# Scores of the first self attention on row halves of the array, weighted sums in pairs, projections from split rows

## What is computed

```python
h = _layernorm(x, ln1_g, ln1_b)
q = (h @ wq).reshape(B, S, 16, 64)      # wk, wv alike
attn = jnp.einsum('bihd,bjhd->bhij', q, k) * 64 ** -0.5
attn = jax.nn.softmax(attn, axis=-1)
out = jnp.einsum('bhij,bjhd->bihd', attn, v).reshape(B, S, 1024)
x = out @ wo + bo + x
```

## Time and profile before

| | us |
|---|---|
| median of 3 runs | 2029.41 (2028.31 to 2030.17) |
| profiled execution, its own time | 2027.02 |
| its span | 2025.3 |
| granted TensorE clock, mean | 0.964 |
| PE busy | 1851.6 (91%) |
| DVE busy | 1157.2 (57%) |
| POOL busy | 879.0 (43%) |
| ACT busy | 781.4 (39%) |

### The profile page before, as it was taken

The page is one execution under the profiler, slowest core; times in us unless marked ns, Lnnn a source line. Parts: engine busy times, 40 slices in busy tenths (PEclk is TensorE's granted clock), DMA queues, the critical chain, the costliest instruction groups (busy, mean ns, idle before and its releaser), DMA issues. The chain is left out here.

```text
span 2025.3 us, 27798 instructions
## 1 busy us (share of the span) xinstructions
PE 1851.6 (91%) x8972; PEld 1078.1 (53%) x8972; DVE 1157.2 (57%) x2195; ACT 781.4 (39%) x1300; POOL 879.0 (43%) x767
## 2 busy tenths in 40 slices
PE   4999999999999999979899999996798976898799
PEld 1444444444444444438555577885444434665678
DVE  4666666666666666633566433244688853687601
ACT  2344444444444443441344313221266663344340
POOL 2366666666666666661122300111146655366110
PEclk9999999999999999989999899997699998999899
DMA  1422222232323232203000001103244421000001
GB/s 52 107 62 53 61 54 67 62 70 62 70 62 70 62 70 62 63 24 94 24 1 1 1 3 48 28 10 53 51 70 77 87 48 28 9 1 1 29 16 42
DMA packets 64798, 93.99 MB, mean 46 GB/s; under 512 B 20992, under 2 KB 47132, under 8 KB 64703
## 3 DMA queue, kind: packets, MB, share of 16 engines
q1 hardware_dynamic: 60351, 86.20, 18.9%
q0 software_dynamic: 4352, 6.56, 1.5%
HBM read 22.84 MB, written 2.24 MB: 12 GB/s over the span
## 5 line engine op out<-in xcount | busy, mean ns | idle before, releaser
L1181 POOL TENSOR_TENSOR x<-x,sa_p_buf 128x1024 f32<-128x1024 f32 x192 | 455.2, 2371 | 165.7 <-ACT sa_p_buf L1029 157.7
L1029 ACT ACTIVATE sa_p_buf<-sa_score 128x512 f32<-128x512 f32 x512 | 277.7, 595 | 304.7 <-PE sa_score L956 304.5
L1092 DVE TENSOR_REDUCE sa_mx<-sa_front 128x1 f32<-128x512 f32 x512 | 319.4, 680 | 98.9 <-PE sa_front L930 98.9
L956 PE MATMUL sa_score<-sa_q_stage,sa_k_stage 128*128 128x512 f32 x1024 | 323.9, 438 | 0.0
L970 PE MATMUL sa_out<-sa_p_buf,sa_v_buf 128*64 128x512 f32 x1024 | 275.7, 617 | 0.0
L956 PEld LDWEIGHTS sa_score<-sa_q_stage,sa_k_stage 128*128 128x128 f32 x1024 | 177.8, 189 | 102.9 <-issue 71.3
L528 ACT ACTIVATE sa_p_buf<-sa_score 128x1024 f32<-128x1024 f32 (+1 forms) x160 | 141.1, 938 | 89.9 <-PE sa_score L476 89.8
L1668 POOL TENSOR_TENSOR x<-x,bias_out 128x1024 f32<-128x1024 f32 x24 | 55.7, 2348 | 275.5 <-POOLq L1853 239.3
L342 DVE TENSOR_REDUCE sa_mx<-sa_front 128x1 f32<-128x512 f32 (+1 forms) x256 | 155.9, 650 | 26.4 <-PE sa_front L283 23.3
L1181 POOL TENSOR_TENSOR x<-sa_p_buf 128x1024 f32<-128x1024 f32 x32 | 77.9, 2433 | 155.1 <-ACT sa_p_buf L1029 155.1
L1557 POOL TENSOR_TENSOR ca_probs<-ca_s_sb,ca_inv 128x616 f32<-128x616 f32 x64 | 77.9, 1218 | 125.7 <-DVE ca_inv L1491 125.7
(11 more groups left out here) (177 smaller groups left out, 2892.3 us busy)
## 6 DMA issues: line engine op xcount, KB each, us to landing
sa_k_stage<-sa_k_hi SPq DMA_DIRECT2D x64, 256.0 KB, 4.3
sa_q_stage<-sa_q_hi SPq DMA_DIRECT2D x64, 256.0 KB, 5.1
sa_k_stage<-sa_k_lo SPq DMA_DIRECT2D x32, 256.0 KB, 4.8
sa_q_stage<-x SPq DMA_DIRECT2D x32, 256.0 KB, 5.0
x<-in_x SPq DMA_DIRECT2D x8, 512.0 KB, 7.3
sa_q_stack<-sa_hi SPq DMA_DIRECT2D x64, 64.0 KB, 2.3
sa_k_stack<-sa_hi SPq DMA_DIRECT2D x64, 64.0 KB, 2.4
ff_w<-in_L_xattn_ff_w SPq DMA_DIRECT2D x16, 128.0 KB, 2.1
```

What stands on the lines that cost most here:

```text
L956: mm = pe.matmul(score_ps[n % NSCORE][:], k_stage[:, b, j, part, kt * P:(kt + 1) * P], q_stage[:, b, j, part, h * HALF:(h + 1) * HALF], st ...
L1029: nc.scalar.activation(p_buf[:, s % NPB, j, :], score_ps[n % NSCORE][:], ACT.Exp, scale=SCALE).then_inc(exp_done, 1)
L1092: dve.tensor_reduce(mx[:, b, j, qt, half:half + 1], front_ps[bank(item, j)][:], AX.X, ALU.max).then_inc(drained, 1)
L1181: nc.gpsimd.tensor_tensor(acc[:, h], prev, cur, ALU.add).then_inc(added, 1)
```

## The change

1. `scores` reads q and k where the projections leave them: `q_hi`, `q_lo`, `k_hi`, `k_lo` [128, B, T], head j on rows 64j to 64j+63. The stages, their 12 transfers a body and their clearing go. A step now has 3 products per head of shape (64, 128), the heads side by side on the two row halves, and a fourth, 2 rows by 128 columns, that adds minus the maximum (`one_rows`, `m_rows`). In the built program the instructions of this fourth product carry the tile size (32, 128), at rows 0 and 64 of the array; those of the other three carry (64, 128).
2. Steps go in 8 pairs (`UNITS`): m, scores 2u, m, scores 2u+1, (m), then both weighted sums of the pair before, then the other items.
3. Projections take 6 fp32r matmuls (L896) of split weights and split `hT`, in place of 2 fp32 ones. `hT` is split once, at the start (ACT, then DVE for chunks 0 and 1, POOL for 2 and 3); the weights once a group.
4. 3 banks for items, 4 for scores (before 4 and 3). An m item waits for both its banks before its first matmul. The items ahead of the first body have an order of their own, `first_front`.
5. `load_top(pool, 1)` moves from the end of `pf0` to the start of the second attention.

```diff
-            pool.wait_ge(cleared, B)
-            load_top(pool, 1)
...
-    NBANK = 4
-    NSCORE = 3
+    NBANK = 3
+    NSCORE = 4
...
+        0: [("c", ("m", 5, 1)), ("c", ("m", 6, 1)), ("n", ("k", 0))],
+        1: [("c", ("m", 7, 1)), ("c", ("t", 1)), ("n", ("q", 0)), ("p", ("den", 1))],
+        2: [("n", ("m", 0, 0)), ("n", ("m", 1, 0)), ("n", ("k", 1))],
+        3: [("n", ("m", 2, 0)), ("n", ("m", 3, 0)), ("n", ("q", 1))],
+        4: [("n", ("m", 0, 1)), ("n", ("m", 1, 1)), ("n", ("v", 0))],
+        5: [("n", ("m", 2, 1)), ("n", ("m", 3, 1)), ("c", ("den", 0))],
+        6: [("n", ("m", 4, 0)), ("n", ("m", 5, 0)), ("n", ("t", 0))],
+        7: [("n", ("m", 6, 0)), ("n", ("m", 7, 0)), ("n", ("m", 4, 1)), ("n", ("v", 1))],
...
+    first_front = [("k", 0), ("q", 0), ("k", 1), ("m", 0, 0), ("m", 1, 0), ("m", 2, 0), ("m", 3, 0), ("m", 0, 1), ("m", 1, 1),
+                   ("m", 2, 1), ("m", 3, 1), ("q", 1), ("t", 0), ("v", 0), ("v", 1), ("m", 4, 0), ("m", 5, 0), ("m", 6, 0),
+                   ("m", 7, 0), ("m", 4, 1)]
...
+                    parts = [(ws[:, a, kd, :], hs[:, kd, tokens(c)]) for kd in range(KD)
+                             for ws, hs in ((w_hi, h_hi), (w_hi, h_lo), (w_lo, h_hi))]
+                    for n, (ws, hs) in enumerate(parts):
+                        mm = pe.matmul(fr[:], ws, hs, start=(n == 0), stop=(n == len(parts) - 1))
...
+                    wait_free(g, b, item, 0, ("q", qt // QH), ("k", half))
+                    wait_free(g, b, item, 1)
...
+                    for part, (ks, qs) in enumerate(((k_hi, q_hi), (k_hi, q_lo), (k_lo, q_hi))):
+                        for j in range(G):
+                            r = slice(dh * j, dh * j + dh)
+                            pe.matmul(score_ps[(s * G + j) % NSCORE][:], ks[r, b, keys], qs[r, b, queries], start=(part == 0),
+                                      stop=False, skip_group_check=True)
+                    for j in range(G):
+                        r = slice(dh * j, dh * j + 2)
+                        pe.matmul(score_ps[(s * G + j) % NSCORE][:], one_rows[r, :], m_rows[r, b, queries], start=False,
+                                  stop=True, skip_group_check=True).then_inc(score_full, 1)
...
+                    for u in range(UNITS):
+                        tops = owned(u, g, b, "m")
+                        for of, item in tops[:1]:
+                            front_item(*of, item)
+                        scores(g, b, 2 * u)
+                        for of, item in tops[1:2]:
+                            front_item(*of, item)
+                        scores(g, b, 2 * u + 1)
+                        for of, item in tops[2:]:
+                            front_item(*of, item)
+                        if u >= 1:
+                            weighted(g, b, 2 * u - 2)
+                            weighted(g, b, 2 * u - 1)
```

More of the change, by code:

```diff
@@ L732, in is_last, with splits @@
         return isinstance(g, int) and (g, b) == (NG - 1, 1)
+    def splits(g, b):
+        return b == 0 and not (isinstance(g, int) and g == NG - 1)
     def before(g, b):
@@ L746, in owner, with owned @@
         return None if is_last(g, b) else after(g, b)
+    def owned(u, g, b, kinds):
+        return [(owner(who, g, b), item) for who, item in lanes[u] if item[0] in kinds and owner(who, g, b) is not None]
     def sums(s):
@@ L816, in out_cols, with tokens @@
             return oT[:, g, at] if isinstance(g, int) else oT[:, bass.ds(g, 1), at].squeeze(1)
[L818 to L840, removed]
+        def tokens(c):
+            return slice(c * HALF, (c + 1) * HALF)
         NPROJ = 4
@@ L881, in both @@
                     g2, b2 = after(g, b)
-                    front(g2, b2, g2 + 1 if b2 == 1 and not is_last(g2, b2) else None)
+                    maxima(g2, b2, 0)
+                    if b2 == 1 and not is_last(g2, b2):
+                        sp.wait_ge(drained, drained_count(g2, b2, ("v", 1)))
+                        load_v(g2 + 1)
                 load_qk(0)
@@ new lines, in values @@
+                def values(g, b, item):
+                    fr = front_ps[bank(item)]
+                    if item == ("v", 0):
+                        pe.wait_ge(wv_in, (g + 1) * DMA)
+                    for t in range(4):
+                        at = b * T + (item[1] * 4 + t) * P
+                        for kd in range(KD):
+                            mm = pe.matmul(fr[:, t * GD:(t + 1) * GD], hT[:, kd, at:at + P], wv[:, kd, :],
+                                           start=(kd == 0), stop=(kd == KD - 1))
+                    mm.then_inc(front_full, 1)
@@ new lines, in maxima @@
+                def maxima(g, b, item):
+                    _, qt, half = item
+                    wait_free(g, b, item, 0, ("q", qt // QH), ("k", half))
+                    wait_free(g, b, item, 1)
+                    for j in range(G):
+                        r = slice(dh * j, dh * j + dh)
+                        pe.matmul(front_ps[bank(item, j)][:], q_hi[r, b, qt * P:(qt + 1) * P],
+                                  k_hi[r, b, half * HALF:(half + 1) * HALF], start=True, stop=True).then_inc(front_full, 1)
@@ L972, in weighted @@
                     mm.then_inc(pv_done, 1)
-                def denominators(g, b, h):
-                    pe.wait_ge(added, lin(g, b, NADD, (KT - 1) * (h + 1)))
-                    wait_free(g, b, ("den", h), 0)
-                    for j in range(G):
-                        mm = pe.matmul(front_ps[bank(("den", h))][64 * j:64 * j + 64, :], ones[:, 0:64], acc[:, h, j, :],
-                                       start=True, stop=True)
-                    mm.then_inc(front_full, 1)
-                def front(g, b):
-                    for s in range(STEPS):
-                        for who, item in lanes[s]:
-                            if who == "n":
-                                front_item(g, b, item)
@@ L988, in both, with front @@
[L988 to L1002 removed]
+                def front():
+                    for item in first_front:
+                        front_item(0, 0, item)
@@ new lines, in both @@
+                def both(g, b):
+                    for u in range(UNITS):
+                        tops = owned(u, g, b, "m")
[10 more added lines that the diff above has]
+                            weighted(g, b, 2 * u - 1)
+                        elif not is_first(g, b):
+                            weighted(*before(g, b), STEPS - 2)
+                            weighted(*before(g, b), STEPS - 1)
+                        for of, item in owned(u, g, b, ("q", "k", "v", "t", "den")):
+                            front_item(*of, item)
```

300 lines of the change are left out of this document (139 added, 161 removed).

## The result

The changed kernel takes **2105.32 us** (median of 4 runs, 2099.44 to 2108.73), the kernel before 2029.79 (median of 4 beside it): ratio 1.0372, 95% interval 1.0342 to 1.0401. The forecast was slower, 2057 in a range of 2018 to 2074. The sign is right; the size is not, +76 us in place of +28. One of the four runs of the kernel before was in a slow state (2193.62 us); the three others lie between 2028.31 and 2030.17.

What follows compares the result with a forecast made beforehand. PE's own queue was taken to bound the first attention; +20 us for 15 bodies, +11 front and -3 restart on the profiled 2027.0 gave 2055, as median 2057, range 2018 to 2074, slower at 0.68.

Steps and rivals of the forecast that it cites:

- What bounds the kernel: First attention: PE's own queue takes the time, PE nearer 100% busy at full clock, a body 52.87 us.
- Product streams 0: Score products in a body: four full-array matmuls become four side-by-side pairs on row halves, 64 streams before and now: 0.
- projections -1.4: Projections in a body: six fp32r matmuls at 0.227 us replace four fp32 records at 0.43, four times: -1.4 us.
- weighted sums in pairs: Shape changes in a body: 9 into weighted sums and den against 16 before, at 0.15 us each.
- The deciding term: Shape changes in a body: passages between 64 and 32 rows cost 0.2 us each, +2.15; without them -2.85.
- The first two rivals: Passages between 64 and 32 rows cost nothing (chance 0.17, median 1996 us), or only half is paid (0.09, 2026 us).
- Waits, 1.65 a body: PE's bank waits in pairs 2, 3, 4 and 7 sum to 1.65 us a body against 1.2 before: +0.45.
- +1.3: Sum per body of projections, shape changes, separate transpose and waits: +1.3 us, over 15 bodies +20 us.
- Front, +11: Ahead of the first body: split weights, bank waits and 2 us for half clock add 11 us (6 to 16).
- Last body 0: Last body: no items for a next one, POOL's sums set the end and PE's extra lies under them: 0.
- Restart -3: Second attention's restart after `pf0`: without POOL's eight issues it moves from POOL's end to DVE's, -3 us.
- Rival of no bank waits: In the bodies DVE catches up and the bank waits are absent: median 2032 us, chance 0.06.

Runs made afterwards that it cites:

- 64 rows: Changed kernel with the product that subtracts the maxima over 64 rows of each half in place of 2: 2102.88 us, ratio to before 1.0377.
- the two kernels with short additions: Changed kernel with GpSimd adding only 8 of 512 columns (denominators wrong): 2058.99 us; the same with the product of the maxima on 64 rows: 2007.96 us.
- the last two kernels of the join: Changed kernel, join by reductions and ScalarE, weight split on GpSimd, m mostly one step later: 2053.94 us; plus 64 rows and single waits in the front: 1968.73 us.
- single waits: Changed kernel in whose front each matmul of a maxima group waits for its own bank only: 2097.86 us, ratio to before 1.0353.
- The experiment on the front: Changed kernel with single waits ahead of the first body: 2097.86 us, ratio to before 1.0353.
- m later: Changed kernel with the maxima groups one step later on TensorE in pairs 0 to 6: 2140.4 us, ratio to before 1.0557.
- the one without waits: Changed kernel with join by reductions and ScalarE, weight split on GpSimd, m mostly one step later: 2053.94 us; 1968.73 with 64 rows and single waits in the front.

## Why the prediction was right in sign and wrong in size

*What bounds the kernel*: right for the kernel before, where the profile names no wait of PE from 100 to 850 us. For the changed kernel it holds only with the waits: 5 us of PE's work a body taken away (64 rows) gave nothing, because VectorE's chain, held up by GpSimd, set when PE could go on.

*Product streams 0, projections -1.4 (my sum gives it as what is saved, +1.4), weighted sums in pairs*: right. Six projection matmuls and the change behind them take 1.59 (394.21 to 395.80).

*The deciding term, passages between 64 and 32 rows at 0.2*: right in size. A 2-row pair takes 0.43 to the next group (381.73 to 382.16); the 64-row product removed the 0.2. The count was right too: 49 changes of shape a body, 25 of them between 64 and 32 rows. Over a whole body less comes back than 0.2 each: less the named waits, the two kernels with short additions take 54.1 - 1.45 and 51.1 - 1.93 us, 3.5 us for 25 passages or 0.14 each, and the last two kernels of the join 4.9 us for 31, or 0.16. The first two rivals are out.

*Waits, 1.65 a body*: **this is the step that failed.** Those I named are there with their sizes: 0.49 in pair 2, 0.45 in pairs 3 and 4. But I let the split of weights "delay DVE by 0.69", a duration from a stage in which POOL rests, and left the join out, as if a queue's operations kept their durations when they are moved. In their place the runs show VectorE held up by GpSimd: the copy of the join takes 2.23 us, and with short additions 0.17 and the body 54.09. Of the 4.4 us a body, 54.1 - 52.9 = 1.2 are what I forecast (+1.3). The join's waiting adds 55.9 - 54.1 = 1.8. The split adds 1.3 to every second body, 0.65. The rest, 57.27 - 54.1 - 1.8 - 0.65 = 0.7, goes with the clock: bodies of 60.7 and 60.3 at 0.94, where others of the same kind take 57.2.

*Front, +11*: mis-sized, 14.6. For the m groups' waits I had 2.0 and 1.3; single waits make the front 5.9 shorter. And the first body, which I took as any other, adds 9.3, at a granted clock of 0.91 (82.67 to 132.33) where before it was 1.00 (68.05 to 108.43). The experiment on the front shows that the two belong together.

*Last body 0*: right. *Restart -3*: the mechanism was right, the size 5.8. I moved the restart by the distance between the ends of the two engines, 2.94. But before, the next stage starts its first transfer 3.12 us behind POOL's last issue (1396.03 to 1399.15), and in the kernel after 0.28 behind DVE's last operation (1478.15 to 1478.43): that difference of 2.8 is what I lacked. Why POOL's issues take so much longer to be followed is not shown.

*Rival of no bank waits*: out. None of my rivals had an engine that holds up another, and the range ended at the bounds of terms that I had listed. (Their sum is 2041.4 to 2072.4; I printed 2042 to 2073, and nothing hangs on it.)

## What to carry to other kernels

An operation that keeps its place in VectorE's queue doesn't keep its duration: when a change shifts the phase of two engines, mark each VectorE copy from SBUF, operation with a scalar from SBUF and operation on two SBUF tensors, and look what GpSimd does at that moment. Short operations at the head of a chain are the ones to move to a reduction or to ScalarE. And judge an edit with such waits gone: the 64-row product gave nothing on the kernel after, and 4.9 us a body on the one without waits.

## What was unexpected of the hardware

- VectorE operations that waited for GpSimd's 2.4 us additions: on two SBUF tensors (8 elements, 1.0 on average, 1.9 in the row shown; 512 elements, 2.5 for 0.68), copy (2.2), with a scalar (2.2), with a scalar and a tensor (2.3). Not so: reduction from SBUF to SBUF (0.170), reciprocal (0.92 in all traces), and whatever reads PSUM (0.692 for a subtraction of 512 elements).
- In some bodies of the kernel after stretches at the lower clock stand between the waits (granted 0.94 over 132.32 to 193.04), in others of the same kind not (1.00 over 365.10 to 422.29). From 200 to 760 us the granted clock was 1.00 in the kernel before, with short additions and in the last two kernels of the join, 0.99 in the kernel after, 0.97 with 64 rows and 0.95 with m later, where PE's longest waits were 1.2, 3.4 and 2.8 us. Why only some bodies fall, no run here settles.
